# Windowed attention in a software pipeline: probabilities divided before the value product, values as the stationary operand

## The reference, cut to what matters

```
def attn_layer(x, Wqkv, qs, ksc, Wo):
    q, k, v = split(x @ Wqkv)               # 16 heads of 64
    q = l2norm(q) * qs ; k = l2norm(k) * ksc
    q, k = rotary(q), rotary(k)
    out = local_attention(q, k, v)
    return out @ Wo

def local_attention(q, k, v):               # windows of 32, each looks at itself and the one before
    sim = einsum('bhwie,bhwje->bhwij', bq, bk2) * 8
    sim = where(mask, -big, sim)
    attn = softmax(sim, -1)                 # 32 rows, 64 columns per window
    return einsum('bhwij,bhwje->bhwie', attn, bv2)
```

## Time and profile before

| | us |
|---|---|
| median of three runs | 2221.41 (2220.75 to 2226.19) |
| the profiled execution | 2223.47, its span 2221.4 |
| time mix (from the span's start) | about 330 |
| layers' pipeline | 330 to 2205 |
| last norm and store | 2205 to 2221 |
| PE busy over the span | 1906.4 (86%) |
| DVE busy | 1633.4 (74%) |
| POOL busy | 1456.0 (66%) |
| ACT busy | 1157.2 (52%) |

### The profile page before, as it was taken

How to read it: one execution, slowest core, us unless ns; L and a number is a source line. 1 busy time by engine, 2 the same in 40 slices (tenths; PEclk the granted TensorE clock), 3 DMA queues, 4 the chain that set the end, 5 groups by cost and what they waited for, 6 DMA issues and landing times. The chain is left out here.

```text
span 2221.4 us, 87355 instructions
## 1 busy us (share of the span) xinstructions
PE 1906.4 (86%) x34160; PEld 1376.1 (62%) x34160; DVE 1633.4 (74%) x3442; ACT 1157.2 (52%) x2034; POOL 1456.0 (66%) x1150
## 2 busy tenths in 40 slices
PE   6777757899999998999898999999998989999985
PEld 4555534666666666666666666666666666666664
DVE  5777766777777777777777777777777777777764
ACT  1111113566655666656565655656565656655652
POOL 0000016877777778777777777778777777777771
PEclk5555558999999999999999999999999999999997
DMA  4000002222232222322222222223222223222220
GB/s 136 1 0 0 0 0 49 59 58 55 54 83 72 60 57 57 85 64 64 53 54 53 80 72 60 57 57 85 66 65 53 54 53 87 65 58 57 57 57 19
DMA packets 93565, 123.18 MB, mean 55 GB/s; under 512 B 27760, under 2 KB 41808, under 8 KB 93392
## 3 DMA queue, kind: packets, MB, share of 16 engines
q1 hardware_dynamic: 93232, 122.42, 21.8%
q10 hardware_dynamic: 288, 0.13, 0.0%
HBM read 20.74 MB, written 1.05 MB: 10 GB/s over the span
## 5 line engine op out<-in xcount | busy, mean ns | idle before, releaser
L884 POOL TENSOR_TENSOR across<-unit,turns 128x512 f32<-128x512 f32 x384 | 526.6, 1391 | 323.9 <-issue 312.8
L892 POOL TENSOR_TENSOR rotated<-along,across 128x1024 f32<-128x1024 f32 x192 | 494.7, 2576 | 20.4 <-POOL along L918 9.6
L1035 DVE TENSOR_REDUCE sums<-squares 128x16 f32<-128x1024 f32 x192 | 234.2, 1220 | 271.3 <-ACT squares L940 271.3
L988 ACT COPY o_t<-att 128x512 f32<-128x512 f32 x192 | 103.2, 589 | 247.5 <-PE att L1131 247.5
L1131 PEld LDWEIGHTS turn<-identity,rotated 128*128 128x128 f32 x1536 | 172.4, 141 | 93.2 <-issue 81.0
L1131 PE MATMUL turn<-identity,rotated 128*128 128x128 f32 x1536 | 204.8, 276 | 28.2 <-POOL rotated L892 28.2
L918 POOL TENSOR_TENSOR along<-unit,turns 128x1024 f32<-128x1024 f32 x96 | 226.9, 2363 | 0.0
L1236 PE MATMUL proj_a<-w_qkv,shift_a 128*128 128x512 f32 x384 | 189.2, 615 | 37.1 <-issue 36.2
L1261 PEld LDWEIGHTS att<-o_t,w_o 128*128 128x128 f32 x1536 | 188.2, 193 | 6.1 <-issue 1.0
L1164 PE MATMUL proj_a<-w_qkv,shift_a 128*128 128x512 f32 x384 | 186.1, 608 | 4.0 <-POOL shift_a L872 2.6
L1261 PE MATMUL att<-o_t,w_o 128*128 128x128 f32 x1536 | 188.5, 276 | 0.0
(11 more groups left out here) (182 smaller groups left out, 3741.8 us busy)
## 6 DMA issues: line engine op xcount, KB each, us to landing
v_win<-val SPq DMA_DIRECT2D x1536, 64.0 KB, 2.0
w_qkv<-wqkv_dram SPq DMA_DIRECT2D x18, 512.0 KB, 3.9
w_o<-wo_dram SPq DMA_DIRECT2D x6, 512.0 KB, 4.2
where<-positions_dram SPq DMA_DIRECT2D x1, 2048.0 KB, 11.6
w_ffn<-ffn_dram SPq DMA_DIRECT2D x12, 170.5 KB, 2.3
w_ffn<-ffn_dram SPq DMA_DIRECT2D x6, 192.0 KB, 2.3
x_tok<-x_dram SPq DMA_DIRECT2D x4, 256.0 KB, 4.5
out_dram<-final SPq DMA_DIRECT2D x4, 256.0 KB, 2.4
```

The costliest lines, as they stand in the source:

```text
L884: pool.tensor_tensor(a[:, :, 1 - half, :], u[:, :, half, :], table, ALU.mult)\
L892: pool.tensor_tensor(rotated[j][:, :, :], along[j][:, :, :], across[j][:, :, :], ALU.add).then_inc(rotated_in[j], 1)
L1035: dve.tensor_reduce(sums[:, j, :], squares[j][:, :, :], AX.X, ALU.add).then_inc(summed[j], 1)
```

## The change

1. `heads_out` and its two DVE products (L1041) go, and so do the eight PE transposes of it (L1229) in every step.
2. The DVE multiplies the 128x1024 `probs` by the inverse mass (one instruction, both inputs in SBUF) into `shares`, right behind the reciprocal and ahead of `hidden`.
3. The transposes of the probabilities, now of `shares`, move on PE from the opening of the step to behind the k projection; the q projection opens the step. ACT's `p_t` copies move behind the squares of k.
4. The mix moves behind the transposes of k. Its stationary operand is now the 64x64 block of `v_win`, its moving operand 32 columns of `p_t`, its output 64 partitions by 32 columns: as many matmuls as before, in two positions of the array (rows and columns 0 to 63, rows and columns 64 to 127) where there were eight. The output is already the transposed layout that `o_t` needs, so ACT copies it directly, one half after four head pairs and one after eight. Both positions write the same bank (`a_ // 4`); before, each row half had a bank of its own.
5. In odd steps ACT runs an exponential of one column behind the `k_t` copies, so that the table load for the exponential stands there.

```diff
 # DVE, opening of the step (live["b"])
-                        after(dve, scaled_out, 2 * b)
+                        after(dve, shared, b)
                         dve.reciprocal(inv_mass[:, :], mass[:, :]).then_inc(mass_inverted, 1)
+                        dve.wait_ge(mass_inverted, b + 1)
+                        after(dve, p_turned, 2 * b)
+                        dve.tensor_tensor(shares[:, :, :, :].rearrange("p a b c -> p (a b) c"),
+                                          probs[:, :, :, :].rearrange("p a b c -> p (a b) c"),
+                                          inv_mass[:, :].unsqueeze(2).broadcast_to([128, HEADS, 2 * WINDOW]),
+                                          ALU.mult).then_inc(shared, 1)
...
-                    if live["b"]:
-                        divide_out(0)
-                        divide_out(1)
 # ACT
-                        after(act, p_turned, 2 * a)
-                        after(act, massed, a)
+                        after(act, shared, a)
                         act.activation(probs[:, :, par, :], logits[:, par, :, :], ACT.Exp).then_inc(weighed, 1)
...
+                    if live["down"]:
+                        after(act, warmed, h)
+                        act.activation(warm[:, :], ones[:, 0:1], ACT.Exp).then_inc(warmed, 1)
...
-                            act.wait_ge(o_turned, 2 * b + j + 1)
+                            act.wait_ge(mixed, 2 * b + j + 1)
 # PE
-                    if live["b"]:
-                        pe.wait_ge(weighed, 2 * b + 2)
-                        after(pe, xb_ready, b)
-                        stand_alone(pe, passed)
-                        for j in range(2):
-                            transposes(bank_s[:, j, :], probs_flat, j, p_turned)
...
 # behind the k projection
+                        pe.wait_ge(shared, b + 1)
+                        after(pe, xb_ready, b)
                         stand_alone(pe, passed)
+                        for j in range(2):
+                            transposes(bank_s[:, j, :], shares_flat, j, p_turned)
...
 # behind the transposes of k
+                        pe.wait_ge(p_laid, 2 * b + 2)
+                        pe.wait_ge(v_spread, 256 * b + 256)
...
-                                    mm = pe.matmul(bank_s[WINDOW * w:WINDOW * w + WINDOW, par, HEAD * a_:HEAD * a_ + HEAD],
-                                                   p_t[rows, a_, WINDOW * w:WINDOW * w + WINDOW],
-                                                   v_win[mine][rows, w, HEAD * a_:HEAD * a_ + HEAD], start=True, stop=True)
-                                    if (a_, w) == (PAIRS - 1, BLOCKS - 1):
-                                        mm.then_inc(mixed, 1)
+                                    mm = pe.matmul(bank_s[rows, a_ // 4, at + WINDOW * w:at + WINDOW * w + WINDOW],
+                                                   v_win[mine][rows, w, HEAD * a_:HEAD * a_ + HEAD],
+                                                   p_t[rows, a_, WINDOW * w:WINDOW * w + WINDOW], start=True, stop=True)
+                            if a_ % 4 == 3:
+                                mm.then_inc(mixed, 1)
...
-                    if live["b"]:
-                        pe.wait_ge(scaled_out, 2 * b + 2)
-                        for j in range(2):
-                            transposes(bank_s[:, j, :], heads_flat, j, o_turned)
```

More of the change, by code:

```diff
@@ L746, in layers @@
         p_t = sb("p_t", [128, PAIRS, TILE])
-        heads_out = sb("heads_out", [128, PAIRS, 2, HEAD])
+        shares = sb("shares", [128, PAIRS, 2, 2 * WINDOW])
         o_t = sb("o_t", [128, PAIRS, TILE])
@@ L758, in layers @@
         hidden = sb("hidden", [128, NC_, TWO])
+        warm = sb("warm", [128, 1])
+        warmed = sem("warmed")
         cleared, centre_made = sem("cleared"), sem("centre_made")
@@ L775, in layers @@
         massed, mass_inverted = sem("massed"), sem("mass_inverted")
[L776 to L777 removed]
+        p_turned, p_laid, mixed, shared = sem("p_turned"), sem("p_laid"), sem("mixed"), sem("shared")
+        o_laid, attended, xb_ready = sem("o_laid"), sem("attended"), sem("xb_ready")
         f_shifted, dev_made, deviated, dev_squared = (
@@ L955, in step @@
                                            bias=w_ffn[0:size, F_B1G + i:F_B1G + i + 1]).then_inc(gelued, 1)
-                    if live["b"]:
-                        for j in range(2):
-                            act.wait_ge(p_turned, 2 * b + j + 1)
-                            after(act, mixed, 2 * b)
-                            act.copy(p_t[:, 4 * j:4 * j + 4, :], bank_s[:, j, :].rearrange("p (a t) -> p a t", t=TILE))\
-                                .then_inc(p_laid, 1)
                     if live["p"]:
@@ L971, in step @@
                         square(1)
+                    if live["b"]:
+                        for j in range(2):
+                            act.wait_ge(p_turned, 2 * b + j + 1)
+                            after(act, mixed, 2 * b)
+                            act.copy(p_t[:, 4 * j:4 * j + 4, :], bank_s[:, j, :].rearrange("p (a t) -> p a t", t=TILE))\
+                                .then_inc(p_laid, 1)
                     if live["a"]:
@@ L1135, in _ @@
                 rotated_flat = [r[:, :, :].rearrange("p h e -> p (h e)") for r in rotated]
-                probs_flat = probs[:, :, :, :].rearrange("p a b c -> p (a b c)")
-                heads_flat = heads_out[:, :, :, :].rearrange("p a b e -> p (a b e)")
+                shares_flat = shares[:, :, :, :].rearrange("p a b c -> p (a b c)")
                 diag_flat = rstd_diag[:, :, :].rearrange("p a t -> p (a t)")
@@ L1207, in step @@
                             transposes(bank_t[:, j, :], rotated_flat[1], j, k_turned)
+                    if live["b"]:
+                        pe.wait_ge(p_laid, 2 * b + 2)
+                        pe.wait_ge(v_spread, 256 * b + 256)
+                        stand_alone(pe, passed)
+                        for a_ in range(PAIRS):
+                            at = TILE * (a_ % 4)
+                            for w in range(BLOCKS):
+                                for par in range(2):
+                                    rows = slice(HEAD * par, HEAD * par + HEAD)
+                                    mm = pe.matmul(bank_s[rows, a_ // 4, at + WINDOW * w:at + WINDOW * w + WINDOW],
[3 more added lines that the diff above has]
+                                mm.then_inc(mixed, 1)
                     if live["a"]:
```

15 lines of the change are left out of this document (removed).

## The result

The kernel after takes 2504.57 us (median of 4 runs, 2500.67 to 2514.38) against 2222.23 for the kernel before on the same chip: ratio 1.127, 95% interval 1.1235 to 1.1313. The direction was forecast, the size wasn't: 282 us slower where 101 were expected, and 75 us above the range. The profiled execution is of 2501.14 us, span 2498.1.

The account below looks back on a forecast made before the run. PE, POOL and DVE were taken to form one loop, DVE and POOL excluding each other. Round 7.6+18.95+13.6 = 40.15 us against 38.0, +101 us over 47.5 rounds, gave 2323 us; range 2236 to 2430.

Parts of the forecast that it names:

- step 5: Even output projection to the next k projection: `along` asks at U'+7.0, `hidden` ends at U'+13.1, k projection starts at U'+13.6.
- Step 2: Odd step on DVE: `along` asks at U+7.9, `shares` asks at U+11.25, the sums start at U+12.55.
- Step 3: POOL's last `rotated`, delayed 0.95 us by `shares`, ends at U+14.9; the even step's k transposes wait for it.
- Step 4: The even step's sums, root and `unit`: U+18.3, plus 0.65 us of root delay by POOL, gives U' = U+18.95.
- a lost race: Rival, 15%: in step 5 the root isn't delayed, `along` and `shares` come behind POOL's work; round 42.0, 2411 us.
- The lock: DVE operations with two SBUF inputs, such as `shares`, start when POOL's current one ends and delay POOL by 0.95 us.
- The mix: On PE, 64 weight loads per position at 0.053 us, positions side by side: 3.5 us with the tail, 1.56 before.
- a rival in which they take turns: Rival, 8%: the mix's two positions take turns, mix 6.9 us, round about 45.4, 2571 us.
- Gains: Division leaves DVE (1.2 us net), eight transposes leave PE (0.9), 0.92 stall goes; k projection to `unit` for q 7.6.
- `shares` doesn't exclude POOL: Rival, 16%: `shares` takes 1.0 us whenever asked; 2240 us with a mix of 3.5 (9%), 2178 with 1.5 (7%).
- The mix is as short as now: Rival, 6%: the odd `along` gets the port at U+7.5, `shares` ends 0.65 us earlier; round 38.85, 2262 us.
- Table load: ACT's load for the exponential moves under the mix; an exponential was never last in the loop, so worth nothing.

Follow-up runs that it names:

- the wait filled: Kernel after plus four unread 512-column matmuls on PE ahead of its wait for `hidden` in odd steps: 2443.08 us, ratio 1.0989.
- the early table: Kernel before with only the one-column exponential behind the copies of `k_t` in odd steps: 2222.44 us, ratio 0.9998.
- the run in quarters: Kernel after with each mix matmul split in two of 32 value channels, 256 instructions in four array positions: 2851.04 us, ratio 1.2818.
- the run with the old mix: Kernel after with only the mix in the shape of the kernel before, output not transposed and so not the reference's: 2372.7 us, ratio 1.0683.
- the mass in PSUM alone: Kernel after with the inverse mass written to PSUM, so that `shares` has one SBUF input: 2284.17 us, ratio 1.0269.
- `hidden` first as well: Kernel after with the inverse mass in PSUM and the `hidden` block ahead of mass, reciprocal and `shares` on DVE: 2238.57 us, ratio 1.0075.
- the last version: Kernel after with inverse mass in PSUM, `hidden` first, the old mix, head outputs turned on PE, and POOL's `rstd_f` behind its last `rotated`: 2167.51 us, ratio 0.9747.
- both moves, old mix: Kernel after with `hidden` first, inverse mass in PSUM and the mix as before, output not transposed and so not the reference's: 2163.24 us, ratio 0.9736.

## Why the prediction was wrong, and where it was right

The step that failed is step 5, and in it the time at which `along` asks; U and U' are the ends of `unit` for q in the odd and in the even step. The forecast had U'+7.0, 0.4 us ahead of the end of `rotated`; it asked at U'+7.49 (1229.57 less 1222.08), and `rotated` ended at U'+7.38. Where the 0.49 come from, in the order of the steps:

- Step 2: `shares` asks at U+11.35 (forecast 11.25) and ends at U+12.5 (12.55), with U = 1203.13.
- Step 3: the last `rotated` ends at 1217.93, U+14.8 (14.9).
- Step 4: U' = 1222.08, U+18.95 (18.95). The sum holds, its parts less: the root was delayed by 0.29 instead of 0.65 (2.42 us from its first operation to `unit`, where it takes 2.13 undisturbed; in most rounds 2.6), and the second sum came 0.3 later, as it waited for squares.
- Step 5: the even output projection comes at U+24.05 (23.6). The mix takes 3.85 us from start to start instead of 3.5, its 64 loads per position 60 ns each instead of 53; the transposes ahead of it 1.02 instead of 0.9; band matmul to v projection 0.08 more; the last `rotated` of step 3, 0.1 early, takes that much back.

So the term that was mis-sized is the mix, by 10%, and it turned over a race that was decided by 0.4 us; but only together with the small ones. With the forecast's 3.5 us, and all else as measured, `along` would have asked at U'+7.14 and won; with 3.85 and the other terms as forecast it would have been a tie (U'+7.03 and 0.35, against 7.38). That a mix shorter by 0.35 us wins in the kernel itself is worked out and not run. From there the time follows; the 2.5 us are the rival's later start of `hidden`, U'+14.3 instead of U'+11.8:

| | round | us |
|---|---|---|
| forecast | 40.15 | 2323 |
| race lost: 2.5 x 47.5 = 119 | 42.65 | 2442 |
| measured with the wait filled, most rounds (mean of all 42.48) | 42.66 | 2443.1 |
| clock, measured against that run | | +61.5 |
| after, most rounds (mean of all 43.66) | 44.2 | 2504.6 |

The rival "a lost race" was the right mechanism with the right place, for another reason: it had the root come early, while U' came when forecast and PE came late. Its round of 42.0 was 0.65 short, as it took no delay of the root; the round on DVE and POOL is 18.95 either way. I gave it 15%, though the forecast itself said that `along` was 0.4 us from losing, on a mix known only from a row at half clock. Both it and the range left out a second failure that follows from the first: PE's wait of 3.56 us costs its clock. The forecast named a granted clock under 0.9 as a cause that it didn't count on; in the layers it was 0.96, and that cost 61 us. A wait on the loop was priced at its length alone.

The other points:

- *What bounds.* Right that DVE and POOL hold the loop beside PE. POOL's chain from `unit` to the last `rotated` is 13.95 us before, 13.96 with the early table, and when 0.42 us of it are gone, the rounds at full clock shorten by 0.24.
- *The lock.* Right: one SBUF input less, and it is gone. The Trainium skill, "SBUF — State Buffer", section "Who interferes with whom", says that a DVE instruction with at most one SBUF input doesn't contend with GpSimd. The trace agrees: 1.22 us each time beside a `rotated` of 2.36.
- *The mix.* The two positions run side by side, as assumed; that the loads set their pace fits the run in quarters, but isn't separated from the matmuls. 3.92 us (3.85 from start to start) against 3.5. The Trainium skill, "TensorEngine Tiling (Array Packing)", section "Restrictions and Gotchas", says that row tiles can't access one PSUM bank simultaneously, from which the forecast made a rival in which they take turns. The trace doesn't bear that out for this kernel: turns would be 6.9 us by the forecast's count. The output halves lie on different partitions of the bank.
- *Gains.* K to U at full clock is 7.65 us in the run with the old mix (1201.50 to 1209.15), forecast 7.6. The band's stall went.
- *`shares` doesn't exclude POOL.* The run that makes this world, the mass in PSUM alone, took 2284.2 us where the rival had 2240: `hidden` behind `shares` was still waited for (0.79 us). With `hidden` first as well it is 2238.6, and 2163.2 with the short mix (forecast 2178); the rival didn't count on that move, so this nearness is luck.
- *The mix is as short as now.* Its 38.85 us, 1.3 under the forecast where `shares` gives back 0.65, come out only with no delay of the root. The root took 3.22 us instead of 2.13; the rounds that began at full clock took 40.1, and the run 2372.7 us where the rival had 2262.
- *Table load.* Nothing, as forecast, but for another reason (above).
- *Signs to look for.* These came: an idle time of over 2 us ended by `hidden`, one of 1.14 ended by `rotated`, `rotated` 0.8 us longer, no stall ahead of the band. These missed their bounds: `shares` at 3.23 us (2.4 at most), the mix at 3.92 (3.6), the step at 21.8 us (20.1).

Left open: why the clock falls in about every second round behind waits of 2.06 us, and what holds POOL for 0.22 us in the last version.

## What to carry to other kernels

Where two engines exclude each other, write down for each request how far it is from the end of the other's operation; if that is less than the error of any term ahead of it, both outcomes belong in the range with nearly equal weight, and so does what a long wait does to PE's clock. Look at which operands make the lock: here a 16-column operand in PSUM instead of SBUF was worth 220 us of 282, and moving the gating operation ahead of the contested one 216, both together 266. A stall that vanishes on PE is no gain while another engine's chain holds the round; the way to gain is to shorten that chain. When a run comes out faster, count the rounds at full and at lowered clock apart: a shorter wait can gain more by the clock than by its length.

## What the runs showed of the hardware that I had not expected

- PE's granted clock falls to 0.50 after a wait of 3.56 us, in about every second round after one of 2.06, in 20 of 49 after one of 1.57 (both moves, old mix), and in 8 of 47 after one of 1.17 in the last version (windows view, the 2 us behind that wait, which had 1.00 in front of it):

```profile
1246.00:1248.00 2.00, 2.00 (x44) 1.67 (x47) 1.79 (x7) 0.98 (x2) 1.64 (x4) 0.61 0.27 66
```

- A PE loop with 128 more matmuls in a step brought idle times of up to 2.9 us for which the profile shows no releaser, 7.70 MB on the instruction queue instead of 0.49, and 346 us more than the kernel after.
- Two row halves of the array wrote one PSUM bank, on different partitions, without taking turns: 3.85 us for 128 matmuls, 60 ns per weight load of 64 columns with its matmul. No run has the same mix in two banks, so a smaller cost of the common bank isn't excluded.
